# A placement rule for side work, and three paths taken off TensorE, in a two-layer kernel of attention and feed-forward blocks

## The reference, cut to what matters

```python
x = x + 0.5 * ffn0(layernorm(x))     # x W^T + b + (x V) C^T, folded into one 128x128 weight
x = x + attn0(layernorm(x))          # 16 heads of 8; q, k l2-normalized; two rounds (below)
x = x + 0.5 * ffn0(layernorm(x))
x = x + 0.5 * moe(layernorm(x))      # 8 experts, top 2, and a shared expert, hidden 128
x = x + attn1(layernorm(x))          # 16 heads of 8, block mask, softmax
x = x + 0.5 * moe(layernorm(x))
# the two rounds of attn0:
state = q
for _ in range(2):
    att = softmax(einsum('bqhd,bkhd->bqhk', state, k))
    state = einsum('bqhk,bkhd->bqhd', att, v)
```

## Time and profile before

| what | value |
|---|---|
| median of 3 runs | 3888.49 us (3873.29 to 3897.85) |
| the profiled execution | 3882.77 us, its span 3881.0 us |
| mean granted TensorE clock | 0.927 of full |
| busy share of the span | PE 87%, weight loads 44%, DVE 61%, ACT 56%, POOL 27% |
| matmul instructions | 20374 |

### The profile page before, as it was taken

How to read it: one execution, slowest core, us unless ns; L and a number is a source line. 1 busy time by engine, 2 the same in 40 slices (tenths; PEclk the granted TensorE clock), 3 DMA queues, 4 the chain that set the end, 5 groups by cost and what they waited for, 6 DMA issues and landing times. The chain is left out here.

```text
span 3881.0 us, 55455 instructions
## 1 busy us (share of the span) xinstructions
PE 3390.9 (87%) x20374; PEld 1726.9 (44%) x20374; DVE 2382.1 (61%) x5217; ACT 2157.3 (56%) x2817; POOL 1063.2 (27%) x2225
## 2 busy tenths in 40 slices
PE   4888888898998989898998989899898989988887
PEld 2334343344444434444453444444344444444454
DVE  2335565666756666675766667576766757566573
ACT  1444566565565655556566655566665555664432
POOL 3122213141422314141231414133231413212231
PEclk7789799898999989999998989899998989998898
DMA  1000000000000000000000000000000000010110
GB/s 37 1 1 28 4 28 4 28 29 31 27 28 29 4 31 28 31 29 31 25 7 28 29 31 29 31 26 7 28 28 31 29 31 26 7 50 4 53 31 31
DMA packets 71259, 95.85 MB, mean 25 GB/s; under 512 B 40304, under 2 KB 58160, under 8 KB 70864
## 3 DMA queue, kind: packets, MB, share of 16 engines
q1 hardware_dynamic: 70992, 92.29, 7.4%
HBM read 82.76 MB, written 4.78 MB: 23 GB/s over the span
## 5 line engine op out<-in xcount | busy, mean ns | idle before, releaser
L734 ACT ACTIVATE probs<-ps 128x1024 f32<-128x1024 f32 x1536 | 1574.6, 1025 | 979.8 <-PE ps L598 944.4
L897 DVE TENSOR_REDUCE negmax<-ps 128x2 f32<-128x1024 f32 x1024 | 1251.9, 1223 | 740.0 <-PE ps L639 731.2
L598 PE MATMUL ps<-qT,kT 32*128 32x512 f32 x3072 | 811.5, 524 | 326.7 <-ACT probs L734 307.8
L615 PE MATMUL ps<-probs,v 128*32 128x512 f32 x6144 | 885.7, 651 | 0.0
L598 PEld LDWEIGHTS ps<-qT,kT 32*128 32x128 f32 x3072 | 300.4, 192 | 1008.2 <-ACT probs L734 644.4
L1105 POOL TENSOR_TENSOR xe<-xT_m,G 128x512 f32<-128x512 f32 x288 | 368.6, 1283 | 1103.1 <-PE ps L676 879.8
L676 PE MATMUL ps<-xe,w_sb 128*128 128x256 f32 x2304 | 648.8, 407 | 19.9 <-POOL xe L1105 14.4
L639 PE MATMUL ps<-kT,qT 32*128 32x512 f32 x2048 | 549.0, 531 | 66.4 <-DVE negmax L897 66.4
L676 PEld LDWEIGHTS ps<-xe,w_sb 128*128 128x128 f32 x2304 | 405.0, 195 | 252.3 <-issue 174.4
L764 ACT ACTIVATE th<-ps 128x256 f32<-128x256 f32 x576 | 221.9, 385 | 337.1 <-PE ps L676 334.1
L962 DVE SCALAR_TENSOR_TENSOR th<-th,ps 128x256 f32<-128x256 f32 x576 | 238.7, 414 | 225.2 <-ACT th L764 212.8
(11 more groups left out here) (170 smaller groups left out, 2900.6 us busy)
## 6 DMA issues: line engine op xcount, KB each, us to landing
G<-gates_dram SPq DMA_DIRECT2D x96, 768.0 KB, 6.2
v<-v_tok SPq DMA_DIRECT2D x256, 18.0 KB, 1.9
X<-in_x SPq DMA_DIRECT2D x16, 256.0 KB, 8.1
out<-X SPq DMA_DIRECT2D x16, 256.0 KB, 2.3
w_sb<-in_w SPq DMA_DIRECT2D x1, 1152.0 KB, 5.5
w_sb<-in_w SPq DMA_DIRECT2D x1, 576.0 KB, 6.4
gates_dram<-gT SPq DMA_DIRECT2D x32, 18.0 KB
wqkv<-in_wqkv SPq DMA_DIRECT2D x2, 192.0 KB, 2.5
```

Source lines behind the costliest of these rows:

```text
L598: nc.tensor.matmul(ps[:, B_ST + h, :], kT[a][rows, g * S + kc * P:g * S + (kc + 1) * P], qT[a][rows, g * S:(g + 1) * S], start=True, stop= ...
L615: ins = nc.tensor.matmul(ps[ROWS * j:ROWS * (j + 1), B_UT, :], v[:, at:at + ROWS], probs[:, n % QUADS, j, :], start=(kc == 0), stop=(kc == ...
L734: nc.scalar.activation(probs[:, quad % QUADS, j:j + 2, :], ps[:, B_ST:B_ST + 2, :], ACT.Exp).then_inc(sem["exp_done"], 1)
L897: nc.vector.tensor_reduce(negmax[job_no(kind, b, g) % 2][:, tc, 2 * half:2 * half + 2], ps[:, B_SM:B_SM + 2, :], AX_X, ALU.max, negate=Tru ...
```

## The change

Five things change.

1. **Placement.** Each event gets a cost in slots (`COST`: `st` 0.22, `pv` 0.48, `m_gu` 0.47, `m_down` 0.28, a group of four transposes 0.25, `sm` 0). A side event may enter a slot only if the slot's sum stays within 1.3 (`OVER`), for `m_gu` and `m_down` within 1.0 (`FULL`); else it moves to the next. An event can be tied to stay `behind` another by a distance, so that what depends on a moved event moves along.
2. **S1 to S2 state.** The four `turn` and four `state` transposes of an S1 window leave PE, and the two copies leave ACT. DVE transposes PSUM bank 4 in blocks of 32x32, divides, writes the stack and transposes it back; POOL copies it into `qT`.
3. **Maxima.** The four `rows` transposes leave PE, and the spreading copy and the add leave DVE. DVE transposes the 32 columns of maxima, SP issues four small transfers into one row per head (`maxrow`), and POOL adds them into `qT`. The constants of the L1 keys change to match.
4. **Start.** The block of its own is gone. Loads come in three groups in order of use, the first x behind the first group; the foldings are ten events of the timeline (four at the very front, six in turn 0), the masks one; POOL fills the zeros at the head of its list.
5. **First turns and warming.** Turns 0 and 1 are 72 and 80 positions long, with windows closer together; no `warm` matmuls are left. The last turn's positions shift along, with the expert lead 18 positions instead of 16.

```diff
-UNIT = 1.75
+PV_AT = 3.3
...
+FFN0_AT, P0_AT, P0_OP_AT = -37, -28.5, (-11, -9, -5, 2)
+O0_AT, MOE0_AT, UNIT0, P1_AT = 5, 30, 1.75, 69
+O1_AT, MOE1_AT, UNIT1 = 85, 80, 1.75
+EARLY = 2
+TURNS = [72, 80] + [TURN] * NB
+STARTS = [sum(TURNS[:i]) for i in range(NB + 4)]
+EARLY_S1_AT, EARLY_S2_AT, EARLY_MAX_AT = (0, 8, 16, 24), (32, 42, 52, 62), (16, 26, 36, 46)
+EARLY_MOE0_AT, EARLY_UNIT, EARLY_P1_AT = 27, 1.1, 58
+END = STARTS[NB]
+L1_END = {NB - 2: tuple(END + i for i in (10, 20, 30, 40)), NB - 1: tuple(END + i for i in (90, 100, 110, 120))}
 L1_MAX_END = 14
 UNIT_END = 1.1
-OUT1_END = {NB - 2: LAST + TURN + 52, NB - 1: LAST + TURN + 132}
-MOE0_END = LAST + TURN + 24
-P1_END = LAST + TURN + 55
-MOE1_END = {NB - 3: LAST + TURN + 54, NB - 2: LAST + TURN + 84, NB - 1: LAST + TURN + 149}
-SIDE_EVENTS = frozenset("ffn_xt ffn_y p0_xt p0_qkv p0_op turn state rows o_t o_y m_xt m_logits m_gt m_gu m_down "
-                        "p1_xt p1_qkv p1_op warm".split())
+OUT1_END = {NB - 2: END + 52, NB - 1: END + 132}
+MOE0_END = END + 24
+P1_END = END + 55
+MOE1_END = {NB - 3: END + 54, NB - 2: END + 84, NB - 1: END + 149}
+WARM = ()
+COST = {**{n: 0.25 for n in "ffn_xt p0_xt p1_xt o_t m_xt p0_op p1_op turn m_gt m_logits".split()},
+        "ffn_y": 0.48, "o_y": 0.48, "p0_qkv": 0.36, "p1_qkv": 0.36, "m_gu": 0.47, "m_down": 0.28, "warm": 0.22,
+        "fold": 0.7, "st": 0.22, "sm": 0.0, "pv": 0.48}
+FULL, OVER = 1.0, 1.3
+FILLERS = ("m_gu", "m_down")
+FOLD_AT = (-50, -48, -46, -44, 8, 11, 14, 17, 20, 23)
+MASKS_AT = 26
...
+    def at(self, pos, name, *args, behind=None):
+        if behind:
+            self.behind[(name,) + args] = behind
         self.marks.append((pos, len(self.marks), name, args))
...
+            if key in self.behind:
+                other, gap = self.behind[key]
+                ready = placed[other] + gap if other in placed else pos + 0.5
+                if pos < ready:
+                    put_back((ready, i, name, args))
+                    continue
...
+                slot = int(pos // 1)
+                now = load.get(slot, 0)
+                if now + COST[name] > (FULL if name in FILLERS else OVER):
+                    put_back((slot + 1.05, i, name, args))
+                    continue
+                if pos < slot + min(now, 0.9):
+                    put_back((slot + min(now, 0.9), i, name, args))
+                    continue
+                if name == "m_down" and args[-1]:
...
+                load[slot] = now + COST[name]
+                if load[slot] > FULL:
+                    load[slot + 1] = load.get(slot + 1, 0) + load[slot] - FULL
+                ends[bank] = pos + max(LAG[e].get(name, 0) for e in ("act", "dve"))
...
-        if b == 0 and kind != "L1" or b == 1 and kind == "S1" or b == NB - 1 and kind == "L1":
-            t.at(start + i + 0.5, "warm", kind, b, g, i)
...
-    t.at(start + 11.2, "turn", kind, b, g)
     if kind == "S1":
-        t.at(start + 14.2, "state", b, g)
+        t.at(start + 11.2, "state", b, g)
+    else:
+        t.at(start + 11.2, "turn", kind, b, g)
...
+    t.at(start, "m_stats", b, k, behind=(("o_y", b, 1) if k else ("ffn_y", b, 1), 1))
...
+        t.at(units + 2 * unit * e - 2, "m_xe", b, k, e, 
+             behind=(("m_gu", b, k, e - 2, 1), 0.8) if e >= 2 else (("m_gt", b, k), 3.5))
         for h in range(2):
-            t.at(units + unit * (2 * e + h) + 0.5, "m_gu", b, k, e, h)
+            t.at(units + unit * (2 * e + h) + 0.5, "m_gu", b, k, e, h,
...
+        early, last = b < EARLY, b == NB - 1
+        t.at(t0 - 60 if b else FOLD_AT[0], "load", b)
+        ffn_events(t, t0 + FFN0_AT, b, 0)
+        p = t0 + P0_AT
...
+            window(t, t0 + (EARLY_S1_AT if early else S1_AT)[g], "S1", b, g)
+            window(t, t0 + (EARLY_S2_AT if early else S2_AT)[g], "S2", b, g)
+            max_job(t, t0 + (EARLY_MAX_AT if early else S2_MAX_AT)[g], "S2", b, g)
...
+            [(weff[:], ffn_wT), (vT, ffn_vT), (cT, ffn_cT), (id_sb[:], ident), (bffn[:], ffn_b.partition_broadcast(P))],
+            [(wqkv[0][:], wqkv0), (lnw_sb, lnw), (lnb_sb, lnb), (bqkv[0][:], bqkv0.partition_broadcast(P)),
+             (bo[0][:], bo0.partition_broadcast(P))],
+            [(con[:], consts), (wqkv[1][:], wqkv1), (wo[0][:], wo0), (wo[1][:], wo1), (gate_w[:], gateT),
+             (bqkv[1][:], bqkv1.partition_broadcast(P)), (bo[1][:], bo1.partition_broadcast(P)),
+             (pairs_i[:, 0, :], src.partition_broadcast(P)), (pairs_i[:, 1, :], tgt.partition_broadcast(P)),
+             (w13_flat, w13), (w2_sb[:], w2)],
...
+                if b == 0:
+                    weights(0)
                 sp.dma_start(tok(b)[:], x_dram[b]).then_inc(x_loaded[b % 2], 16)
+                if b == 0:
+                    weights(1)
+                    weights(2)
...
+            def rows(n, kind, b, g):
+                target = maxrow[ADD0::ROWS, :].rearrange("j (t b q) -> j b t q", t=TC, b=NG)
+                sp.wait_ge(sem["mx_ready"], n + 1)
+                if n:
+                    sp.wait_ge(sem["rows_added"], n)
+                for i in range(NG):
+                    sp.dma_start(target[:, i],
+                                 negmaxT[ROWS * i:ROWS * i + NG * TC, :]).then_inc(sem["rows_in"], 16)
...
+            def fold(n, i):
+                key = ("fold", i)
+                if i == 0:
+                    pe.wait_ge(*have(0))
+                elif i == 1:
+                    pe.wait_ge(*read(("fold", 0)))
+                elif i == 2:
+                    pe.wait_ge(*have(1))
+                elif i == 3:
+                    pe.wait_ge(sem["prep"], 1)
+                elif i == 4:
+                    pe.wait_ge(*have(2))
+                    pe.wait_ge(sem["prep"], 2)
...
+                if kind == "S1":
+                    return
+                act.wait_ge(sem["state_done"], states_up_to(n))
...
+            def uts_state(n, kind, b, g):
+                if kind != "S1":
+                    return
+                if no[("state", b, g)]:
+                    dve.wait_ge(sem["state_done"], no[("state", b, g)])
+                dve.wait_ge(sem["pv_done"], TC * (n + 1))
+                nc.vector.transpose(uts[:],
+                                    ps[:, B_UT, :]).then_inc(sem["ut_copied"], 1)
+                dve.wait_ge(sem["ut_copied"], n + 1)
+                link(nc.vector.reciprocal(rden[:], s1t[:, :, HD]))
+                link(nc.vector.tensor_tensor(st8[:], s1t[:, :, 0:HD],
+                                             rden[:].unsqueeze(2).to_broadcast([P, TC * NG, HD]), ALU.mult))
+            def state(n, b, g):
+                twice = qstack[:, :, 0:2 * HD].rearrange("p x (r d) -> p x r d", r=2).bitcast(F32R)
+                link(nc.vector.tensor_copy(twice, st8[:].unsqueeze(2).to_broadcast([P, TC * NG, 2, HD])))
+                link(nc.vector.tensor_tensor(qstack[:, :, 2 * HD:3 * HD].bitcast(F32R), st8[:], qstack[:, :, 0:HD],
+                                             ALU.subtract))
+                nc.vector.transpose(uts[:],
+                                    qstack[:].rearrange("p x e -> p (x e)")).then_inc(sem["state_turned"], 1)
...
-            def rows(n, kind, b, g):
-                key = ("rows", kind, b, g)
-                target = qT[layer(kind)][:, g * S:(g + 1) * S]
-                dve.wait_ge(*filled(key))
-                nc.vector.tensor_tensor(target, side_bank(key), target.bitcast(F32), ALU.add).then_inc(read_signal(key), 1)
-                dve.wait_ge(*read(key))
-                dve.sem_inc(sem["rows_added"], 1)
...
+            def mx_turn(n, kind, b, g):
                 dve.wait_ge(sem["sm_read"], 2 * TC * (n + 1))
-                nc.vector.tensor_copy(mx[:, :, ADD0:ROWS],
-                                      negmax[n % 2][:].rearrange("p c j -> p (c j)").unsqueeze(2)
-                                      .to_broadcast([P, TC * NG, ROWS - ADD0])).then_inc(sem["mx_ready"], 1)
...
+            def state(n, b, g):
+                pool.wait_ge(sem["state_turned"], n + 1)
+                nc.gpsimd.tensor_copy(qT[0][:, g * S:(g + 1) * S],
+                                      uts[:]).then_inc(sem["state_done"], 1)
+            def rows(n, kind, b, g):
+                target = qT[layer(kind)][:, g * S:(g + 1) * S]
+                pool.wait_ge(sem["rows_in"], 16 * NG * (n + 1))
+                nc.gpsimd.tensor_tensor(target, maxrow[:], target.bitcast(F32), ALU.add).then_inc(sem["rows_added"], 1)
```

412 lines of the change are left out of this document (202 added, 210 removed).

## The result

The changed kernel takes 3653.15 us (median of 4 runs, 3644.95 to 3660.7), the kernel before 3890.74 us (4 runs); the ratio is 0.9395, with a 95% interval of 0.9357 to 0.9434. The forecast was 3655 us. The profiled execution has a span of 3654.9 us against 3881.0. The first fence has the stretches of the changed kernel with the columns of the earlier trace rows: turns 0, 1 and 2, turns 3 to 14 together, turn 15, the end turns in two parts.

The account below looks back on a forecast made before the run. The prediction took PE as the bound, with 22.6 us idle in a full turn. Start, turns 0 to 2, twelve full turns at 12 us, turn 15 and the end sum to -233: 3882.8 - 233 + 5.7 = 3655 us, range 3540 to 3800.

Parts of the forecast that it names:

- the 12 us: Gain forecast for each full turn: 8 for transposes, 7 for placement, less 3 for VectorE's bursts; bounds 0 and 34.
- Transposes off PE, 8 us: Full turns: 11.2 us of transposes leave PE, those behind a `pv` gaining all; 8 us a turn, bounds 0 and 11.2.
- Placement, 7 us: Full turns: every `m_gu` moves to a slot without `pv`, filling a third of PE's idle time; 7 us a turn.
- VectorE's new bursts, 3 us: Full turns: DVE's 2.5 us bursts at window ends, with an `sm` queued behind; 3 us lost a turn, bounds 0 and 10.
- rival D: Less busy PE drops to the low clock, sign turn 0 under 0.75 or full turns under 0.90; 3795 us, chance 0.10.
- the 56 us forecast: Turns 0 and 1: shorter turns with windows closer together and no `warm` matmuls; -28 us each, bounds 0 and -45.
- The start, -20: Before turn 0: grouped loads let the first normalization start near 16 us instead of 36.3; 20 us earlier, bounds 12 and 24.
- Turn 2, -10 to +3.4: Turn 2: the forecast term was 10 us less; +3.4 is the measured value.
- The end, +8 to -7.6: End turns: `rows` leave, late maxima and lower clock cost time; forecast +8, bounds 0 and +35; -7.6 is measured.
- The 8 us for late maxima: End turns: the maxima's longer way has a lead of only 3.4 positions; 8 jobs about 1 us late each.
- rival E: Maxima queue on SP behind broadcasts and value transfers, delaying a window's first `st`; 4010 us, slower than before, chance 0.08.

Follow-up runs that it names:

- bothunpl: `bothpe` with the two slot limits lifted from the start of turn 3 to the last 40 positions; 3782.7 us, ratio 0.9747.
- unplaced: The changed kernel with the two slot limits lifted from the start of turn 3 to the last 40 positions; 3741.1 us, ratio 0.9633.
- bothpe: The changed kernel with the S1 state and the maxima both transposed on PE again; 3610.7 us, ratio 0.9286.
- rowspe: The changed kernel with the maxima transposed on PE again, that event left out of the slot limits; 3704.6 us, ratio 0.9521.
- statepe: The changed kernel with the S1 state transposed on PE again, the maxima still off it; 3602.0 us, ratio 0.9257.
- statelate: The changed kernel with the second half of VectorE's state work planned three slots later; 3711.6 us, ratio 0.9541.
- stats: `bothpe` with the statistics of slot 8 (`ffn_stats`) moved behind that slot's score maximum on VectorE; 3576.4 us, ratio 0.9215.
- spfix: `statepe` with SP's order changed so the maxima's transfers are issued ahead of the gates' broadcasts and the value transfers; 3616.0 us, ratio 0.9316.
- sumlate: `stats` with `p0_sums` later on VectorE, behind the maximum of slot 81, and as much later on GpSimd; 3599.7 us, ratio 0.9286.
- warmeven: The changed kernel with 148 extra matmuls of unread output in even slots 0 to 98 and 134 to 180; 3632.5 us, ratio 0.9340.
- best1: `stats` plus the layer 1 scalings as their own event, `warmeven`'s matmuls and two extra pairs in slot 28 of full turns; 3525.8 us, ratio 0.9085.
- best2: `best1` with `sumlate`'s order, without slot 28's extra matmuls, with more such matmuls in turns 2 and 3 and the end; 3546.3 us, ratio 0.9139.

## Why the forecast was right

The time was right to 2 us, and that is in part luck. The errors of the terms run from -16 us (the end) to +13 us (turn 2) and cancel, and in a full turn the 12 us are right while none of the parts is: the runs give -2.2 us from the kernel before to `bothunpl`, -14.0 for the placement and +3.9 for the transposes, where I had -7 and, with VectorE's bursts, -5. This table splits the full turns (mean of turns 3 to 14, us; the low clock's cost is the estimate defined above):

| kernel | turn | low clock costs | rest |
| --- | --- | --- | --- |
| before | 224.2 | 12.2 | 212.0 |
| transposes on PE, unplaced (`bothunpl`) | 222.0 | 9.3 | 212.7 |
| transposes off, unplaced (`unplaced`) | 220.4 | 14.4 | 206.0 |
| transposes on, placed (`bothpe`) | 208.0 | 7.4 | 200.6 |
| state off alone, placed (`rowspe`) | 215.7 | 15.3 | 200.4 |
| maxima off alone, placed (`statepe`) | 209.1 | 9.7 | 199.4 |
| changed: off, placed | 211.9 | 12.3 | 199.6 |
| `statelate` | 216.8 | 17.3 | 199.5 |
| `stats` | 204.9 | 4.6 | 200.3 |

In the six placed kernels of the table the rest stays within 199.4 and 200.6 us while the low clock's part runs from 4.6 to 17.3, which speaks for the estimate. It does not hold for every order: `spfix` has a rest of 201.4 and `sumlate` of 203.1.

- *Transposes off PE, 8 us.* Wrong. Without the clock they give 6.7 us while events crowd the slots of a product (212.7 to 206.0), and 1.0 us once the events are placed (200.6 to 199.6). The step said "those in light slots give nothing" and then counted 8 of 11.2 us; once the placement had evened out the slots, little was left to gain, so my two terms paid for the same idle time. The clock then takes 4.9 us (7.4 to 12.3). Net: 3.9 us lost a turn, VectorE's bursts included, where I had 8 - 3 = 5 gained.
- *Placement, 7 us.* The mechanism is shown: PE's waits for exponentials fall where the limits hold, and no `m_gu` of a full turn stands behind a `pv` any more, where 16 of 36 did. The size is 8.5 us a turn with the transposes off, near my price, and 14.0 with them on. Priced first, with the transposes still on TensorE, it was half of what it is worth.
- *VectorE's new bursts, 3 us.* VectorE's transpose of 128x512 takes 0.71 us, against the 0.68 that I took. The waits for maxima appeared (10.6 us in the stretch shown above), but the rest of a turn is 200.4 us with the state on VectorE (`rowspe`) and 200.6 without (`bothpe`). The difference is in the clock: `rowspe` takes 7.7 us a turn more, the low stretches cost 7.9 more by the estimate and the rest 0.2 less. That longer waits for the maxima bring these stretches is argued, from `statelate` and `stats`; no run takes the waits out of `rowspe`.
- *The clock, rival D.* I gave it .10 and priced it on the early turns and as one jump. It is a part of every kernel here. Turns 0 and 1 fell from 0.81 and 0.92 to 0.68 and 0.80, the first below the 0.75 that I had named as this rival's sign, and still gained 42 of the 56 us forecast. That the closer windows gained it and the missing matmuls took the rest away fits the rows, but no run changes the windows alone. In the full turns the low clock costs the same before and after (12.2 and 12.3 us) only because the rest of the change had saved what the moved transposes then cost: 7.4 us in `bothpe`. The rule named there (the Trainium skill, TensorE: Matmul & The Clock Gate, Part 1), that activity releases the throttle, agrees with `warmeven`, where added matmuls shorten turn 0 from 154.8 to 139.9 us and its clock is 0.88 instead of 0.68.
- *The start, -20.* Measured -17.4. The scalings inside the fourth folding hold up VectorE; taken out, in `best1`, the first exponential comes at 51.2 us instead of 56.95.
- *Turn 2, -10 to +3.4.* It had matmuls for warming in its front before; without them its clock is 0.82. With them, in `warmeven`, it takes 206.8 us instead of 215.8.
- *The end, +8 to -7.6.* The clock of the last windows fell as I had it, from 1.00 to 0.83 (3521.5 to 3596.0 us), and they still took 74.5 us against 78.8, with 354 matmul records instead of 424 once the `warm` ones were gone. The 8 us for late maxima were not paid: over the seven maxima of the end the score matmuls and their weight loads wait 1.2 us in all for GpSimd's add.
- *Maxima late, rival E.* Seen in slots 80 to 83 and small: moving the transfers forward moved the time to the next slots.

What stays open: why the low stretches of `stats` lie at slot 81 alone from turn 4 on, with the 1.1 us wait at slot 28 at the full clock, while in `sumlate` every second turn has one there; and why turn 0 of the same plan takes 150 us in one execution and 163 in another. A kernel with `best1`'s order and the further matmuls of `best2` is not among the runs.
